# One transformer block on one core: a new order of all steps with 585 filler matmuls in place of 428

## The chip, the cores and the metric

The kernel runs on one core of one Trainium2 chip. The metric is the device time of one execution in microseconds (us). Before the change three runs gave 725.46, 726.37 and 730.91 us, median 726.37. Times taken from a profile are of one further, profiled execution.

## The reference

Sixteen sequences of 256 tokens with 128 features go through two layers, each followed by a residual sum and a layer norm without weights. The first is causal attention with 16 query heads of size 8 over 4 key heads, RMS norm and rotary embedding on q and k, and a soft cap of the scores. The second is a whole block: layer norm, full attention with 16 heads over the 256 tokens, a residual, a second norm, and a mixture of 8 experts of which each token takes the one with the largest gate logit.

```python
scores = jnp.tanh(scores / CAP) * CAP                  # first layer, causal, CAP = 50
y = softmax(where(causal, scores, -inf)) @ v @ w_o
x = _layernorm(x + y)
...
hn2 = _layernorm(x2, ln2_g, ln2_b)                     # second layer, x2 = x + attention
idx = jnp.argmax(hn2 @ gate_w + gate_b, axis=-1)
mid = relu(einsum('th,ehf->etf', hn2, w1) + b1)
moe = (einsum('etf,efh->eth', mid, w2) + b2)[idx, arange]
out = _layernorm(x + (x2 + moe))
```

## The kernel before

**The work.** One step of the outer structure is one sequence, called batch n here (16 of them, two tiles of 128 tokens each). The work of a batch is cut into about 130 named steps. The letter of a name is the stage: a_ loads x, projects q, k, v, and normalises and rotates them; b_ makes the first scores, tanh, exp and the causal mask in six pieces; c_ multiplies by v, projects, adds x and norms; d_ projects q, k, v of the second layer and finds each row's maximum score (d_mx on TensorE, d_max on VectorE, eight pieces); e_ makes the second scores and exp in eight pieces; f_ multiplies by v, projects, norms, picks the expert and computes each token's place in a table sorted by expert, and scatters the rows there (f_scatter, an indirect DMA on GpSimd). A plan (p_plan) after batches 7, 11, 14 and 15 then deals out 9, 8, 6 and 17 tiles of 128 rows of one expert each. The g_ steps do one such tile s of 40: g_row fetches its rows, g_w the expert's first weights, g_hT, g_up, g_mid and g_down compute the two matmuls around a ReLU, g_z, g_rs, g_y norm and g_out scatters the result to the output.

**The order.** Each engine has a program of its own: VectorE (DVE), ScalarE (ACT), GpSimd (POOL), TensorE (PE) and SyncE (SP), which issues most DMAs. The table `ORDER` gives each step of each batch a rank. `batch_order` sorts all ranks into one global list, and `pipeline` on each engine goes through it and emits those steps that the engine has. So the table fixes the order of every engine, and the engines meet only through semaphores; nothing on an engine is run before what stands ahead of it.

**Waiting.** TensorE's results go through two rings of two PSUM banks each, ring_p and ring_s. A step takes the next bank of its ring (`claim`), after the step that used it two turns earlier has been read. Attention outputs go to out1 and out2 instead. On GpSimd stand the powers for the RMS norm (a_pow, L1411), for the layer norms (c_pow L1435, f_pow L1460, g_rs L1484), the stacking of heads (L1414) and the causal masks (L1430).

**Fillers.** A step `w_fill` is a matmul of ones into the bank that the next user of ring_p will take, after claiming it; nothing reads its result. It is one matmul of 256 columns on the full array (L701), or, where the last real matmuls were in columns of 32, four of them (L698). The old table has 428 such steps.

**Row fetches.** g_row waits on SP for its plan. The first fetch of each plan also waits until the last two batches' scatters of that plan have landed, the last plan's for the pad rows too. SP also carries the loads of x (a_load), the row maxima into the operand of the e_ scores (d_m, four small DMAs a batch, L632), the weights (g_w) and the pad stores (q_sp, L666).

Of the kernel before, what the change touches and what calls it, by code (L numbers as in the profile page):

```python
# [18 lines left out]
T = S // P  # L19
# [87 lines left out]
def wait_turn(eng, sem, n, buffers, each):  # L107
# [16 lines left out]
    "a_load": (0, 3, 5, 6, 15, 246, 410, 500, 593, 824, 927, 1050, 1226, 1468, 1509, 1684),  # L124
    "a_xTc": (1, 13, 19, 113, 189, 293, 424, 584, 703, 864, 1002, 1187, 1346, 1511, 1634, 1815),
    "a_xT": (2, 7, 17, 70, 165, 257, 392, 534, 693, 865, 987, 1153, 1292, 1497, 1620, 1785),
    "a_qkv": (4, 12, 64, 128, 224, 377, 506, 652, 822, 984, 1093, 1265, 1422, 1593, 1776, 1898),
    "a_rope": (8, 18, 69, 134, 234, 387, 511, 657, 820, 986, 1114, 1270, 1440, 1607, 1791, 1920),
    "a_sum": (9, 20, 81, 139, 245, 389, 513, 665, 842, 1003, 1143, 1272, 1477, 1617, 1805, 1924),
    "w_fill": (10, 29, 30, 42, 49, 60, 67, 88, 99, 100, 112, 136, 152, 154, 159, 164, 169, 181, 185, 197, 202, 203,  # L130
# [198 lines left out]
def post_ln_block(nc, x, w_q, w_k, w_v, w_o, ln1_g, ln1_b, ln2_g, ln2_b, wq, bq, wk, bk, wv, bv, wo, bo,  # L329
                  gate_w, gate_b, w1, b1, w2, b2, c_rope, c_square, c_small, out):  # L330
    with ExitStack() as ctx:
# [250 lines left out]
        for j, (name, n) in enumerate(order):  # L582
# [3 lines left out]
            elif name[:4] in TILE_SHAPE:  # L586
                shape = TILE_SHAPE[name[:4]]
            elif name in ON_TENSOR or name[:4] in ("b_sc", "d_mx", "e_sc"):
                shape = "full"

        def bank(name, n):
            k = ring_of(name, n)
            return ring[k][turn[name, n] % RINGS[k]]
# [927 lines left out]
```

## Time and profile before

| | |
|---|---|
| median of three runs | 726.37 us |
| their spread | 725.46 to 730.91 us |
| span of the profiled execution, first to last instruction | 701.0 us |
| TensorE busy, mean granted clock | 570.1 us (81%), 0.927 |
| VectorE, ScalarE, GpSimd busy | 480.9, 425.4, 416.7 us |
| DMA | 34.30 MB |

The profile gives the span alone; the median of the runs lies 25.4 us above it, which is what lies around the instructions. Busy time of TensorE is of matmuls that overlap in a pipeline. The granted clock is a share of 2.4 GHz: 1.0 is that level, 0.5 is 1.2 GHz. In the chain of waits each piece is what the one after it waited for, or the instruction before it on the same engine. Times of a stretch are microseconds from the start of the span.

### The profile page before, as it was taken

The page shows a single profiled execution, that of the slowest core. Times are in us where ns is not written, and L with a number is a line of the kernel's source. Part 1 is how long each engine was busy: PE and PEld are TensorE (multiplying, and loading weights), DVE is VectorE, ACT ScalarE, POOL GpSimd, SP SyncE. Part 2 cuts the span into 40 slices and gives each one's busy share as a digit, 9 for nine tenths or more (in the row PEclk, how much of TensorE's full clock was granted, in tenths as well). Part 3 has the DMA queues.
Part 4 walks back from the last instruction along what each step waited for, and adds up shares of the span by engine and source line. Part 5 has one row for each costly group of instructions (what it writes and reads, how often), then busy time and mean ns, then how long its engine had stood idle before and what let it go on. Part 6 is the DMA issues. An engine that isn't in the chain of part 4 may idle for free.

```text
span 701.0 us, 16358 instructions
## 1 busy us (share of the span) xinstructions
PE 570.1 (81%) x5771; PEld 339.1 (48%) x5771; DVE 480.9 (69%) x1356; ACT 425.4 (61%) x650; POOL 416.7 (59%) x443
## 2 busy tenths in 40 slices
PE   2648888888888878888897898878997899888992
PEld 1324333344445444455454554545553555557992
DVE  3546757868678868587867768687777787635452
ACT  1675376676785666757677596756675654534661
POOL 2469573648486953775757585769544235525664
PEclk9969779899999988799999999899998999999996
DMA  6420000000000100000012301001002022186650
GB/s 146 135 69 2 8 1 9 2 24 1 9 2 25 40 2 6 5 16 10 17 41 62 85 9 36 1 20 60 25 29 62 12 69 91 39 257 183 187 149 6
DMA packets 30143, 34.30 MB, mean 49 GB/s; under 512 B 6970, under 2 KB 21984, under 8 KB 30064
## 3 DMA queue, kind: packets, MB, share of 16 engines
q1 hardware_dynamic: 26096, 25.53, 12.9%
q0 software_dynamic: 2816, 6.43, 2.6%
q10 hardware_dynamic: 1152, 1.30, 0.6%
q8 instruction: 47, 0.77, 0.5%
q14 instruction: 32, 0.26, 0.1%
HBM read 22.37 MB, written 11.27 MB: 48 GB/s over the span
## 4 chain that ended last, share of the span: by engine, by line
PE 40%; DVE 23%; POOL 16%; issue 10%; ACT 7%; SPq 2%; DMA 1%; POOLq 0%; ACTq 0%; DVEq 0%
DVE mx L1230 10%; PE out L877 6%; POOL rs L1411 5%; PE ring_s L863 3%; POOL stack L1414 3%; PE out L762 3%; PE ring_p L943 3%; PE ring_p L701 3%; PE ring_s L843 3%; POOL p L1430 2%; ACT p L1004 2%; PE ring_p L814 2%; ACT p L973 2%; PE ring_s L749 2%; PE ring_p L931 1%
## 5 line engine op out<-in xcount | busy, mean ns | idle before, releaser
L1230 DVE TENSOR_REDUCE mx<-ring_s 128x4 f32<-128x1024 f32 x128 | 152.8, 1218 | 26.9 <-PE ring_s L843 26.1
L1004 ACT ACTIVATE p<-ring_s 128x1024 f32<-128x1024 f32 x128 | 126.3, 1027 | 38.8 <-PE ring_s L863 38.3
L973 ACT ACTIVATE p<-ring_s 128x1024 f32<-128x1024 f32 x96 | 97.1, 1022 | 38.5 <-PE ring_s L749 38.1
L1411 POOL TENSOR_TENSOR rs<-ms,small 128x40 f32<-128x40 f32 x14 | 94.8, 6772 | 27.6 <-DVE ms L1093 27.3
L1414 POOL TENSOR_SCALAR stack<-stack 128x256 f16<-128x256 f16 (+1 forms) x96 | 65.0, 700 | 75.7 <-DVE stack L1222 42.8
L1430 POOL TENSOR_SCALAR_AFFINE_SELECT p<-p 128x512 f32<-128x512 f32 (+1 forms) x96 | 75.8, 798 | 56.4 <-ACT p L977 56.3
L977 ACT ACTIVATE p<-p 128x1024 f32<-128x1024 f32 x96 | 100.2, 1057 | 0.7
L701 PE MATMUL ring_p<-blank 128*128 128x256 f16 x362 | 80.6, 286 | 5.1 <-ACT t_midT L1037 1.9
L877 PE MATMUL out<-p,v 128*32 128x256 f32 x1024 | 69.8, 400 | 1.3 <-DVE rb L1288 1.2
L843 PE MATMUL ring_s<-kc,qs 32*128 32x256 f16 x512 | 51.2, 281 | 20.2 <-DVE mx L1230 13.0
L863 PE MATMUL ring_s<-qs,kc 32*128 32x256 f16 x512 | 49.4, 290 | 10.1 <-DMA qs<-mT 4.5
L1489 POOL DMA_INDIRECT out<-t_y,t_idx x40 | 41.3, 1034 | 16.4 <-DVE t_y L1380 9.0
L701 PEld LDWEIGHTS ring_p<-blank 128*128 128x128 f16 x362 | 32.6, 103 | 37.9 <-issue 25.3
L762 PE MATMUL out<-p,v 128*32 128x256 f32 x512 | 47.0, 443 | 4.5 <-POOL p L1430 4.1
L749 PE MATMUL ring_s<-qs,kT 32*128 32x512 f16 x192 | 40.0, 422 | 9.7 <-DVE mx L1230 4.5
L1484 POOL TENSOR_TENSOR t_rs<-t_ve,small 128x1 f32<-128x1 f32 x40 | 23.5, 591 | 35.8 <-DVE t_idx L1375 35.5
L943 PE MATMUL ring_p<-w_down,t_midT 128*128 x320 | 44.0, 283 | 0.0
L1478 POOL DMA_INDIRECT routed_rows<-row,pos x32 | 32.9, 1027 | 15.4 <-issue 8.1
L877 PEld LDWEIGHTS out<-p,v 128*32 128x32 f32 x1024 | 29.1, 112 | 26.1 <-issue 11.9
L943 PEld LDWEIGHTS ring_p<-w_down,t_midT 128*128 128x128 f32 x320 | 40.5, 199 | 0.0
L843 PEld LDWEIGHTS ring_s<-kc,qs 32*128 32x128 f16 x512 | 15.3, 94 | 51.7 <-DVE mx L1230 26.4
L1037 ACT ACTIVATE t_midT<-ring_p,b_up 128x128 f32<-128x128 f32 x92 | 26.3, 368 | 21.7 <-PE ring_p L931 20.1
(162 smaller groups left out, 1111.5 us busy)
## 6 DMA issues: line engine op xcount, KB each, us to landing
w_up<-in_L_ffn_w SPq DMA_DIRECT2D x40, 256.0 KB, 2.8
t_row<-routed_rows SPq DMA_DIRECT2D x40, 132.0 KB, 2.4
routed_rows<-padrow SPq DMA_DIRECT2D x8, 396.0 KB, 3.2
xs<-in_L_attn_x SPq DMA_DIRECT2D x16, 128.0 KB, 2.2
routed_rows<-padrow SPq DMA_DIRECT2D x8, 132.0 KB, 1.9
qs<-mT SPq DMA_DIRECT2D x64, 2.0 KB
out<-t_y,t_idx POOLq DMA_INDIRECT x40, 2.4
b_down<-in_L_ffn_b SPq DMA_DIRECT2D x1, 512.0 KB, 4.8
```

Source lines behind the costliest of these rows:

```text
L701: nc.tensor.matmul(spare[:, 0:256], blank[:, 0:P], blank[:, 0:256], start=True, stop=True)
L843: mm = nc.tensor.matmul(bank(f"d_mx{j}", n)[:, z * 512 + g * S:z * 512 + (g + 1) * S], qs2[32 * i:32 * i + 32, n % 2, 2 * k + g, t * P:(t ...
L863: mm = nc.tensor.matmul(bank(f"e_sc{u}", n)[:, j * 512 + v * S:j * 512 + (v + 1) * S], kc2[32 * i:32 * i + 32, n % 2, g, keys * P:(keys + ...
L877: mm = nc.tensor.matmul(out2[32 * c:32 * c + 32, half * S:(half + 1) * S], v2[:, n % 2, keys, 8 * half + 2 * c + v, :], p2[:, u, at:at + S ...
L943: mm = nc.tensor.matmul(bank("g_down", s)[:, 0:D], t_midT[:, s % 2, c * P:(c + 1) * P], w_down[:, bass.ds(e * FF + c * P, D)], start=False ...
L973: nc.scalar.activation(p1[:, u], bank(f"b_sc{u}", n)[:], ACT.Tanh, scale=float(ISQ / CAP)).then_inc(b_s.sem, 1)
L977: nc.scalar.activation(p1[:, u], p1[:, u], ACT.Exp, scale=CAP).then_inc(b_x.sem, 1)
L1004: nc.scalar.activation(p2[:, u], bank(f"e_sc{u}", n)[:], ACT.Exp, scale=float(ISQ)).then_inc(e_s.sem, 1)
L1230: nc.vector.tensor_reduce(mx2[:, t, 2 * pair:2 * pair + 2, 2 * k:2 * k + 2], bank(f"d_mx{j}", n)[:].rearrange("p (z g s) -> p z g s", z=2, ...
L1411: nc.gpsimd.tensor_tensor(rs1[:], ms1[:], half, ALU.pow).then_inc(a_p.sem, 1)
L1414: return nc.gpsimd.tensor_scalar(dst, src, 1.0, None, ALU.mult)
L1430: nc.gpsimd.affine_select(out=w, in_=w, compare_op=ALU.is_ge, fill=0.0, base=0, pattern=[[0, w.shape[1]], [1, P]], channel_multiplier=-1). ...
```

## The change

The whole of `ORDER` is replaced. The 2415 real steps are the same, with other ranks; the fillers are 585 instead of 428, 524 of them on the full array and 61 in columns. The list of a fetch's scatters is now taken from the order: every g_row waits for the latest two f_scatter steps ahead of it, where only the first of a plan waited for fixed ones. All line numbers behind the table are 7 higher, and in the engines' programs 13 or 14 higher: L701 becomes L714, L698 becomes L711.

```diff
-    "w_fill": (10, 29, 30, 42, 49, 60, 67, 88, 99, 100, 112, 136, 152, 154, 159, 164, 169, 181, 185, 197, 202, 203,
...
+    "w_fill": (1, 2, 3, 4, 5, 6, 12, 13, 14, 18, 19, 20, 21, 22, 23, 29, 30, 31, 32, 33, 34, 35, 36, 37, 38, 39, 40,
...
+        scattered, so_far = {}, []
+        for name, n in order:
+            if name == "f_scatter":
+                so_far.append(n)
+            elif name == "g_row":
+                scattered[n] = tuple(so_far)
...
                 sp.wait_ge(r_v.sem, r_v.upto(k, "row"))
+                for n in scattered[s][-2:]:
+                    wait_turn(sp, rows_out[n % 2], n, 2, 16 * T)
                 if s == PLANS[k][1]:
-                    last = PLANS[k][0]
-                    for n in (last - 1, last):
-                        wait_turn(sp, rows_out[n % 2], n, 2, 16 * T)
                     if k >= LAST:
```

The order of TensorE at the very start, before: transposes of x (ring_p<-ident,xs), projections (w_qkv,xT), the stacked heads' transposes (identh,stack) and first scores (qs,kT).

```order
L707 MATMUL ring_p<-ident,xs 128x128 x2
L714 MATMUL ring_p<-w_qkv,xT 128x192 x2
L707 MATMUL ring_p<-ident,xs 128x128 x2
L701 MATMUL ring_p<-blank 128x256
L714 MATMUL ring_p<-w_qkv,xT 128x192 x2
L707 MATMUL ring_p<-ident,xs 128x128 x2
L725 MATMUL ring_p<-identh,stack 128x128 x8
L733 MATMUL ring_p<-identh,stack 128x128 x2
L749 MATMUL ring_s<-qs,kT 128x512 x4
```

The same stretch after:

```order
L714 MATMUL ring_p<-blank 128x256 x6
L720 MATMUL ring_p<-ident,xs 128x128 x2
L714 MATMUL ring_p<-blank 128x256 x3
L727 MATMUL ring_p<-w_qkv,xT 128x192 x2
L714 MATMUL ring_p<-blank 128x256 x6
L720 MATMUL ring_p<-ident,xs 128x128 x2
L714 MATMUL ring_p<-blank 128x256 x13
L727 MATMUL ring_p<-w_qkv,xT 128x192 x2
L714 MATMUL ring_p<-blank 128x256 x6
L738 MATMUL ring_p<-identh,stack 128x128 x8
```

Fillers stand ahead of the first transpose and between all of these steps, 35 before the first scores where one stood; the third transpose of x has moved behind the scores.

TensorE between the last product with v of batch 0 (`ob`, the transposes of its sums, is the step after it) and the first transpose for the second layer (ident,xh), before:

```order
L775 MATMUL out<-ident,sums 128x128 x4
L749 MATMUL ring_s<-qs,kT 128x512 x2
L781 MATMUL out<-ident,o 128x128 x2
L701 MATMUL ring_p<-blank 128x256
L749 MATMUL ring_s<-qs,kT 128x512 x4
L786 MATMUL out<-w_out,oT 128x128 x2
L749 MATMUL ring_s<-qs,kT 128x512 x2
L701 MATMUL ring_p<-blank 128x256 x2
L808 MATMUL ring_p<-ident,xh 128x128 x2
```

After, from the step behind those transposes of the sums:

```order
L714 MATMUL ring_p<-blank 128x256 x13
L794 MATMUL out<-ident,o 128x128 x2
L714 MATMUL ring_p<-blank 128x256 x6
L762 MATMUL ring_s<-qs,kT 128x512 x4
L714 MATMUL ring_p<-blank 128x256
L799 MATMUL out<-w_out,oT 128x128 x2
L714 MATMUL ring_p<-blank 128x256 x3
L762 MATMUL ring_s<-qs,kT 128x512 x2
L714 MATMUL ring_p<-blank 128x256 x6
L762 MATMUL ring_s<-qs,kT 128x512 x2
L714 MATMUL ring_p<-blank 128x256 x6
L821 MATMUL ring_p<-ident,xh 128x128 x2
```

The real steps are nearly the same, the fillers went from 3 to 35 here (and six column fillers stand just ahead of the piece).

TensorE in the last stage, from the output projection of batch 15 (w_out,oT) over the expert matmuls of two tiles (t_hT,w_up) to its gate (w_gate,h2T), before:

```order
L786 MATMUL out<-w_out,oT 128x128 x2
L701 MATMUL ring_p<-blank 128x256
L931 MATMUL ring_p<-t_hT,w_up 128x128 x8
L701 MATMUL ring_p<-blank 128x256
L897 MATMUL out<-ident,row 128x128 x2
L924 MATMUL ring_p<-ident,t_row 128x128
L701 MATMUL ring_p<-blank 128x256
L903 MATMUL out<-w_gate,h2T 128x8 x2
```

After:

```order
L799 MATMUL out<-w_out,oT 128x128 x2
L944 MATMUL ring_p<-t_hT,w_up 128x128 x8
L714 MATMUL ring_p<-blank 128x256 x9
L910 MATMUL out<-ident,row 128x128 x2
L714 MATMUL ring_p<-blank 128x256 x5
L937 MATMUL ring_p<-ident,t_row 128x128 x2
L916 MATMUL out<-w_gate,h2T 128x8 x2
```

Nine fillers stand where one did ahead of the transposes of `row`, five behind them, and one more expert tile's transpose is ahead of the gate.

## Rows read from the trace of the kernel before

**Rows 1.** The page: span; busy us, share and instructions; clock in 40 slices.

```profile
span 701.0 us, 16358 instructions
...
PE 570.1 (81%) x5771; PEld 339.1 (48%) x5771; DVE 480.9 (69%) x1356; ACT 425.4 (61%) x650; POOL 416.7 (59%) x443
...
PEclk9969779899999988799999999899998999999996
```

**Rows 2.** The page: the chain that ended last, by engine and line.

```profile
PE 40%; DVE 23%; POOL 16%; issue 10%; ACT 7%; SPq 2%; DMA 1%; POOLq 0%; ACTq 0%; DVEq 0%
DVE mx L1230 10%; PE out L877 6%; POOL rs L1411 5%; PE ring_s L863 3%; POOL stack L1414 3%; PE out L762 3%; PE ring_p L943 3%; PE ring_p L701 3%; PE ring_s L843 3%; POOL p L1430 2%; ACT p L1004 2%; PE ring_p L814 2%; ACT p L973 2%; PE ring_s L749 2%; PE ring_p L931 1%
```

**Rows 3.** Length, busy PE, PEld, DVE, ACT, POOL, clock of low-clock stretches; fourteen in the sum.

```profile
41.90:55.50 13.60, 5.95 (x31) 2.66 (x29) 4.55 (x14) 7.31 (x9) 11.20 (x8) 0.50 0.26 89
72.60:82.90 10.30, 9.76 (x63) 3.90 (x67) 7.89 (x10) 2.31 (x4) 7.80 (x11) 0.50 0.01 2
...
sum 92.40, PE 79.73 PEld 41.06 DVE 53.21 ACT 49.35 POOL 56.50; mean PE 5.70 PEld 2.93 DVE 3.80 ACT 3.52 POOL 4.04
```

**Rows 4.** The chain between 72.6 and 82.9 us, by engine and line.

```profile
by line: PE ring_p L814 27.7%; PE ring_s L843 21.6%; PE out L762 21.5%; PE ring_p L701 12.5%; DVE mx L1230 11.9%; PE out L767 8.3%; PE ring_p L808 6.0%; issue 0.4%
```

**Rows 5.** TensorE's waits (us in total, times, longest), and the busy times after 690 us.

```profile
PE ring_s L843 <- DVE mx L1230: 13.0, 22, 1.6
PE ring_s L863 <- DMA qs<-mT: 4.5, 5, 1.4
...
690.00:701.00 11.00, 0.00 (x0) 0.00 (x0) 1.35 (x7) 0.00 (x0) 2.66 (x3) 0.52 0.00 0
```

**Rows 6.** The fillers: groups by line, one burst of two, a piece of the chain.

```profile
L701 PE MATMUL ring_p<-blank 128*128 128x256 f16 x362 | 80.6, 286 | 5.1 <-ACT t_midT L1037 1.9 <-DVE qs L1134 1.3 <-ACT t_hT L1027 0.7
...
L698 PE MATMUL ring_p<-blank 128*32 128x256 f16 x264 | 16.7, 291 | 0.1
...
24.91 0.61 PE L701 MATMUL ring_p<-blank 128*128 128x256 f16 x2
...
602.31 0.76 PE ring_p L701 x7
```

**Rows 7.** TensorE in order of time, from the start; all engines from 25 us.

```profile
9.13 0.69 PE L707 MATMUL ring_p<-ident,xs 128*128 128x128 f32 x2 [9.13 <-DMA w_qkv<-in_L_attn_w_v]
10.28 1.65 PE L714 MATMUL ring_p<-w_qkv,xT 128*128 128x192 f32 x4 [0.46 <-ACT xT L968]
15.90 0.69 PE L707 MATMUL ring_p<-ident,xs 128*128 128x128 f32 x2 [3.98 <-DMA xs<-in_L_attn_x]
...
17.05 1.65 PE L714 MATMUL ring_p<-w_qkv,xT 128*128 128x192 f32 x4 [0.25 <-ACT xT L968]
...
21.83 1.03 PE L725 MATMUL ring_p<-identh,stack 128*128 128x128 f16 x8 [2.70 <-POOL stack L1414]
...
26.58 0.61 PE L749 MATMUL ring_s<-qs,kT 32*128 32x512 f16 x2 [0.31 <-ACT p L973]
...
35.12 0.39 PE L749 MATMUL ring_s<-qs,kT 32*128 32x512 f16 x2
...
25.00:30.00 5.00, 2.66 (x9) 0.44 (x9) 2.35 (x9) 5.00 (x6) 2.29 (x5) 1.00 0.14 51
```

**Rows 8.** GpSimd and TensorE in order of time, 42 to 52 us.

```profile
42.59 6.79 POOL L1411 TENSOR_TENSOR rs<-ms,small 128x40 f32<-128x40 f32 x1 [1.69 <-DVE ms L1093]
49.36 1.00 POOL L1435 TENSOR_TENSOR rl<-ve,small 128x4 f32<-128x4 f32 x1
...
51.82 0.69 PE L808 MATMUL ring_p<-ident,xh 128*128 128x128 f32 x2 [7.65 <-DVE xh L1189]
```

**Rows 9.** TensorE in order of time, 622 to 627 us.

```profile
622.91 1.95 PE L931 MATMUL ring_p<-t_hT,w_up 128*128 128x128 f32 x16
625.45 0.28 PE L701 MATMUL ring_p<-blank 128*128 128x256 f16 x1 [0.59 <-ACT t_midT L1037]
626.42 0.44 PE L897 MATMUL out<-ident,row 128*128 128x128 f32 x2 [0.69 <-DVE row L1189]
```

More of the change, by code:

```diff
@@ L123 @@
 ORDER = {
[L124 to L129, printed above, removed]
@@ new lines @@
+    "a_rope": (16, 43, 103, 202, 311, 464, 618, 775, 959, 1106, 1264, 1403, 1585, 1747, 1912, 2023),
+    "a_sum": (17, 44, 111, 211, 317, 491, 619, 779, 975, 1123, 1287, 1425, 1586, 1748, 1925, 2035),
+    "a_root": (25, 66),
+    "a_split": (26, 70, 150, 259, 357, 537, 672, 826, 1015, 1204, 1341, 1507, 1647, 1792, 1960, 2097),
+    "a_stack": (27, 80, 181, 269, 359, 546, 680, 827, 1026, 1205, 1345, 1512, 1671, 1833, 1979, 2112),
+    "a_qT": (51, 83, 191, 276, 363, 576, 696, 857, 1047, 1225, 1366, 1539, 1687, 1834, 1985, 2128),
@@ new lines @@
+    "d_qT": (216, 331, 442, 633, 788, 968, 1132, 1262, 1408, 1582, 1775, 1938, 2036, 2199, 2386, 2525),
+    "p_bT": (217,),
+    "d_qTc": (222, 343, 458, 642, 804, 979, 1141, 1273, 1417, 1584, 1785, 1939, 2042, 2206, 2387, 2528),
+    "d_kT": (225, 338, 446, 635, 799, 974, 1133, 1270, 1411, 1599, 1779, 1942, 2043, 2213, 2395, 2531),
+    "p_bTc": (228,),
+    "d_kTc": (232, 344, 459, 641, 812, 980, 1139, 1274, 1418, 1606, 1783, 1949, 2052, 2224, 2402, 2535),
[16 rows of a table added]
+    "d_nm": (291, 412, 579, 710, 904, 1068, 1201, 1348, 1492, 1670, 1871, 2055, 2166, 2339, 2453, 2582),
@@ new lines @@
+    "f_scatter": (681, 738, 877, 1065, 1253, 1291, 1454, 1590, 1867, 2161, 2230, 2241, 2443, 2546, 2638, 2741),
+    "p_plan": (1574, 2243, 2633, 2734),
+    "g_w": (1603, 1629, 1602, 1914, 1601, 1915, 1728, 1777, 1693, 2389, 2447, 2248, 2250, 2478, 2286, 2288, 2479,
+        2647, 2648, 2657, 2654, 2695, 2658, 2739, 2740, 2744, 2793, 2792, 2822, 2790, 2823, 2833, 2862, 2835, 2868,
+        2876, 2875, 2898, 2940, 2966),
+    "g_row": (1605, 1627, 1628, 1692, 1726, 1727, 1729, 1763, 1776, 2249, 2251, 2252, 2287, 2361, 2371, 2382, 2388,
+        2639, 2649, 2655, 2656, 2688, 2696, 2742, 2745, 2791, 2796, 2797, 2820, 2828, 2834, 2836, 2861, 2863, 2865,
+        2874, 2892, 2895, 2916, 2964),
@@ new lines @@
+    "g_hT": (1634, 1636, 1793, 1853, 1855, 1972, 2032, 2084, 2227, 2326, 2414, 2462, 2502, 2515, 2567, 2568, 2605,
+        2682, 2683, 2719, 2721, 2732, 2764, 2775, 2801, 2804, 2817, 2819, 2838, 2853, 2866, 2880, 2887, 2903, 2912,
+        2922, 2929, 2939, 2951, 2974),
+    "g_hTc": (1651, 1653, 1798, 1854, 1873, 1981, 2038, 2096, 2246, 2328, 2436, 2466, 2509, 2520, 2572, 2579, 2617,
+        2686, 2691, 2723, 2729, 2736, 2776, 2777, 2803, 2814, 2824, 2832, 2840, 2855, 2873, 2885, 2900, 2905, 2917,
+        2925, 2933, 2946, 2957, 2978),
@@ new lines @@
+    "g_rs": (1801, 1872, 1998, 2027, 2160, 2178, 2221, 2242, 2486, 2495, 2545, 2585, 2596, 2635, 2652, 2671, 2700,
+        2731, 2751, 2766, 2779, 2795, 2799, 2827, 2842, 2847, 2858, 2878, 2889, 2896, 2908, 2918, 2930, 2943, 2952,
+        2959, 2968, 2973, 2986, 2997),
+    "g_y": (1830, 1958, 2091, 2126, 2197, 2202, 2223, 2260, 2489, 2499, 2549, 2597, 2601, 2640, 2666, 2679, 2743,
+        2749, 2752, 2768, 2785, 2800, 2815, 2829, 2845, 2860, 2870, 2882, 2894, 2909, 2915, 2924, 2936, 2950, 2955,
+        2967, 2972, 2976, 2987, 2998),
@@ L308 @@
+    "g_out": (1885, 1997, 2162, 2132, 2284, 2302, 2301, 2283, 2505, 2507, 2637, 2653, 2636, 2726, 2737, 2689, 2765,
+        2781, 2754, 2780, 2794, 2821, 2848, 2841, 2871, 2877, 2888, 2890, 2897, 2910, 2941, 2944, 2942, 2953, 2960,
+        2971, 2975, 2977, 2988, 2999),
+    "q_sp": (2693,),
 }
```

146 lines of the change are left out of this document (56 added, 90 removed), and 184 rows, old and new, of the table ORDER.

## The prediction

> **What bounds the kernel now.** I read the page's shares first, then the chain that ended last, then the stretches of low clock, then TensorE's waits.
>
> No engine is full: over the span of 701.0 us TensorE is busy 81% and ScalarE 61% [rows 1]. The chain changes engine all the time: 40% of it is TensorE, 23% VectorE, 16% GpSimd, and 10% is "issue", the small steps between them [rows 2]. So the time is set by the order in which steps meet, with TensorE the most frequent link.
>
> TensorE's clock is granted at the lower of its two levels (0.50, which is 1.2 of 2.4 GHz) in fourteen stretches before the tail. Together they are 92.4 us long, and TensorE is busy in 79.7 us of them [rows 3]. In the one from 72.6 to 82.9 us the chain is nearly all TensorE: its six TensorE entries sum to 97.6% [rows 4]. In the one from 41.9 to 55.5 us TensorE is busy 5.95 of 13.6 us and GpSimd 11.2, so a faster TensorE buys little there. TensorE's idle time is 131 us (701.0 less 570.1), most of it in short waits such as 22 on the row maxima, 13.0 us in all [rows 5]. About 24 us of it are the wait for the first inputs, 9.13 us, the wait for the second x, 3.98 us [rows 7], and the eleven us after the last matmul [rows 5].
>
> **The change, part by part.**
>
> *Fillers: the count.* The program has 428 filler steps before (362 on the full array, 66 in columns of four matmuls) and 585 after (524 and 61, counted in the order of the steps). They stand in 179 bursts after, 270 before; 34 bursts of the new order have exactly six, and three have thirteen. Before, full ones took 80.6 us and the column ones 16.7 us [rows 6]. One more in a burst costs 0.109 us at full clock (seven in 0.76 us) and about 0.21 at half (two end 0.22 us later than one would: 0.61 against 0.39) [rows 6]. So 162 more full ones are 17.7 us at the full clock, 34 at half; five fewer column ones give back about 1. What of this lies on the path: L701 is 3.0% of the span on the chain by the answer behind [rows 2], 21.0 us of its 80.6, or 26%. By that share the new ones cost 0.26 x 17.7 = 4.6 us. The bounds are 0 (every one in a true wait) and 17.7 (none).
>
> *The start.* Six fillers now stand ahead of the first transpose, behind the same wait for w_qkv that ends at 9.13 us [rows 7]. They run at the half clock: the first 35 us show no change of clock and the column says 1.00, but two L749 matmuls take 0.61 us at 26.58 and 0.39 at 35.12 [rows 7]. Six by 0.21 is +1.3 us on the path, since everything of batch 0 follows from that transpose. Three more stand before L714, whose wait was 0.46 us: 0.63 less 0.46 is +0.2. The thirteen ahead of the second L714 take 2.8 us in place of 0.25 us of waiting; but the first tile's stack has to be built meanwhile (TensorE waits 2.70 us for it before L725 [rows 7]), and the second tile is not wanted on ScalarE before the first is through. I charge nothing for them, 1.5 us as the upper bound. The start: +1.5 us.
>
> *What a faster TensorE gives back at the start.* ScalarE is busy for the whole of 25 to 30 us (5.00 of 5.00) [rows 7], so matmuls that run at full clock 15 us earlier shorten nothing there: 0. The Trainium skill ("TensorE: Matmul & The Clock Gate", section "What's actually happening") says that the lower clock is the default and that activity lifts it. The trace agrees: the first matmuls are slow by the durations. By that rule alone the 39 fillers ahead of the third transpose would bring the higher level forward, and half of the matmul time between some 20 and 35 us, about 4 us, could be saved if ScalarE were not full.
>
> *The hole from 42 to 52 us.* Before, TensorE stands idle 7.65 us before L808, behind GpSimd's 6.79 us power and the 1.00 us one queued after it [rows 8]. The new order puts 44 fillers between the last product with v of batch 0 and its projection for the second layer, where 3 stood: 38 full ones are 4.1 us, six column ones 1.5 (16.7/66 each), in about 9 us of waits, so they fit. On VectorE the sum of squares of batch 2 now goes ahead of batch 0's normalisation, so the power that waits for that sum can start sooner by the normalisation's two instructions, but one mask now stands between it and the next power. I cost this at 0. What is gained is that the clock does not fall here.
>
> *Clock.* All 79.7 us at full speed would be half as long: 39.9 us is the upper bound. How much of it is on the path: TensorE holds 40% of the chain at large and 97.6% in the stretch of [rows 4], but little in the first, where GpSimd holds it; I take 60%, 48 us, and halved that is 24. I take it that 60% of the low time goes, 14 us, and not all of it, since between the third batch's transposes and the last maxima of batch 0, where the second stretch fell, the new order has hardly a filler. A third of this is lost to VectorE and ScalarE, which become late next (the maxima hold up TensorE already [rows 5]). The clock: -10 us, between 0 and -40.
>
> *Order.* 2415 real steps keep their work and their dependencies; they move by some 10 to 20 places. The burst sizes show that the order was made with durations near those of the trace: nine fillers (1.0 us) now stand between L931 and L897, where TensorE had one filler (0.28), 0.59 and 0.69 us of waiting [rows 9]. The fetches of rows 20 and 21 and of the weights 19, 20 and 22 now come ahead of the eight pad stores on SP's queue, not behind them. No instruction is added by this, and the last batch still leaves 20 of the 40 expert tiles behind it. What there is to win is 131 - 24 = 107 us of scattered waits, of which an order can win or lose a part: I bound it at 15 us each way and take -5, since bursts fit waits wherever I compared them.
>
> *Row fetches.* Each now waits for the latest two scatters ahead of it in the order. In this order they are always those that its plan already required (6 and 7, then 10 and 11, 13 and 14, 14 and 15), which the first fetch of each plan waited for before too. Behind it on SP stand weight fetches and the 64 small stores of the maxima (4.5 us of waits on them [rows 5]); none waits longer. Cost 0; a microsecond per plan, 4 in all, if the count were one scatter later.
>
> Sum against the profiled span: +4.6 + 1.5 - 10 - 5 = -8.9, some -9 us (adding the column ones back changes it by 0.3), 692. The median of the runs lies 25.4 us over the span, and nothing of the change touches what lies around it: 726.4 - 9 = 717.
>
> **The rivals.**
>
> *Fillers in the way (slower).* A filler is queued in TensorE's order, and it claims the next bank of ring_p: it cannot be skipped when the step behind it is ready early. If the waits for which the bursts were sized are longer than the true ones in the middle of the kernel, where most steps are, the new ones all go on the path: +17.7, the start +1.5, and at most -5 from the clock with nothing from the order: +14, 740. The point from which it decides: once more than about 70% of the new time is on the path while the low stretches shrink by less than a fifth. For it: L701 is already 21 us of the chain. Against it: the fit in [rows 9], and fewer bursts than before.
>
> *A draw.* The low stretches shift and don't shrink (they followed waits on maxima and on GpSimd that no burst of six covers), or VectorE takes all of the gain: -3 + 4.6 + 1.5 = +3; with up to -8 from the order that is 721 to 729, middle 726.
>
> *The clock stays up throughout.* -24 of the clock, -9 of the order, +6.1 for fillers and start: -27, 699. Against it: the same long waits on the 6.8 us powers remain.
>
> *The change doesn't do what it says* in its third part only: the fetches wait for nothing new. That is in my sum already.
>
> **How the numbers follow.** 1% of 726 is 7.3 us, about what a measurement of this kernel can tell from no change. The forecast's own case (711 to 721, middle 717) has 0.36, the clock that stays up 0.12, the draw 0.24, fillers in the way 0.28. Of the forecast's case a tenth, the side of 719 to 721, counts as the same, and of the slower case a tenth too: faster 0.32 + 0.12 = 0.44, same 0.24 + 0.04 + 0.03 = 0.31, slower 0.25. The range leaves a tenth at either end: 696 to 740.
>
> **What would show it.** Right: fewer than 50 us of low clock before the tail; L808's first wait of 7.65 us gone into fillers; the mean of L701 nearer 0.27 us than 0.29; the first transpose still at 9 us but the first score step 1.5 us later; TensorE's busy time about the same or lower although it has 157 fillers more. Wrong: a chain with L714's full filler (its new line) over 5%; low stretches of the same total; or waits of VectorE and ScalarE on TensorE grown. If SP shows a wait for rows_out ahead of fetches 9 or 17 that delays a store of maxima, my zero for the row fetches is wrong.

## The result and the profile after

The kernel after takes 654.79 us (median of four runs, 654.16 to 655.28) against 727.48 us for the kernel before in the same set (725.46 to 730.91): a ratio of 0.9007, 95% interval 0.8977 to 0.9037. It is 73 us faster. Forecast were 717, and a range of 696 to 740: the sign was right, the size about eight times too small (9 us of 73).

The page of the kernel after, which answers to [rows 1] and [rows 2]:

```profile
span 652.3 us, 16677 instructions
...
PE 566.8 (87%) x5913; PEld 351.3 (54%) x5913; DVE 486.9 (75%) x1356; ACT 423.2 (65%) x650; POOL 419.0 (64%) x443
...
PEclk9697588899899999798999999999999999999997
...
PE 44%; DVE 18%; issue 10%; POOL 9%; ACT 6%; SPq 6%; DMA 5%; POOLq 0%; ACTq 0%; DVEq 0%
DVE mx L1243 6%; PE out L890 5%; POOL rs L1424 4%; PE ring_s L856 4%; PE ring_p L714 4%; PE out L775 4%; PE ring_s L876 3%; PE ring_p L956 3%; PE ring_p L827 3%; PE ring_s L762 3%; ACT p L986 2%; SPq L646 2%; ACT p L1017 2%; DMA qs<-mT 2%; PE ring_p L834 2%
```

The engines do the same work in a shorter span, and their busy times hardly change: VectorE is busy 486.9 us, where it was 480.9, GpSimd 419.0 (416.7), and TensorE 566.8 (570.1) although it runs 157 more filler steps. What went is waiting. TensorE's idle time fell from 131 to 85.5 us. In the chain the share of GpSimd fell from 16% to 9%, that of the maxima (mx) from 10% to 6%. The first of these is not steady: the same two programs profiled again have 11% (before_again) and 13% (after_again). SyncE and the DMAs together rose from 3% of the chain to 11% (6% in after_again).

A first correction of the reading of before belongs here. The profiled execution of after has a span of 652.3 us and a time of 654.2: some 2 us lie outside the span, not 25. The profile of before was of a quicker execution than any of its three timed runs. Its 701.0 us would suit the chips on which whole sets of before have medians near 703 us; on which chip it was taken isn't on record. The repeat of before below has a span of 721.7 and a time of 723.4 us, and in other sets the same program had medians from 702.8 to 727.4. So the comparisons of times below are ratios to before on the same chip, or between runs of one chip, unless it is said otherwise.

The low-clock stretches of after ahead of its tail, in the columns of [rows 3], all nine:

```profile
18.20:21.60 3.40, 3.38 (x15) 2.37 (x12) 3.16 (x11) 0.00 (x0) 0.88 (x2) 0.50 1.06 293
25.00:35.30 10.30, 7.58 (x48) 3.21 (x52) 4.26 (x16) 9.52 (x12) 5.21 (x8) 0.50 0.03 12
52.30:59.10 6.80, 5.64 (x26) 2.60 (x26) 4.26 (x8) 2.54 (x3) 6.00 (x9) 0.50 0.00 0
66.00:83.00 17.00, 14.33 (x88) 7.06 (x92) 12.32 (x23) 10.85 (x14) 14.15 (x12) 0.50 0.01 1
93.30:103.50 10.20, 9.54 (x74) 3.90 (x77) 5.31 (x14) 9.13 (x10) 9.48 (x4) 0.50 0.31 100
...
sum 68.10, PE 60.11 PEld 28.73 DVE 39.48 ACT 44.46 POOL 48.55; mean PE 6.68 PEld 3.19 DVE 4.39 ACT 4.94 POOL 5.39
```

68 us are left of 92, and 48 of them lie in the first 104 us; four short ones follow, and none after 308 us. In the repeat of after below it is 65 us in twelve stretches, three of them behind 555 us.

TensorE's and VectorE's waits in after (us in total, times, longest), beside [rows 5] and [rows 8]:

```profile
PE ring_p L821 <- DVE xh L1202: 7.5, 3, 4.6
PE ring_s L856 <- DVE mx L1243: 4.6, 8, 1.1
PE ring_s L762 <- ACT p L986: 4.2, 4, 2.2
...
PE ring_s L876 <- DMA qs<-mT: 3.4, 5, 1.5
```

```profile
DVE t_z L1379 <- PE ring_p L956: 23.6, 21, 3.8
DVE mx L1243 <- PE ring_s L856: 11.3, 24, 1.1
```

The 22 waits of TensorE on the maxima, 13.0 us, are 8 of 4.6 us. The long hole before the first `xh` is not gone, it is 4.6 us where it was 7.65. The fillers:

```profile
L714 PE MATMUL ring_p<-blank 128*128 128x256 f16 x524 | 89.5, 286 | 17.3 <-DMA w_qkv<-in_L_attn_w_v 9.5 <-DVE t_z L1379 2.6 <-ACT t_hT L1040 2.5
L711 PE MATMUL ring_p<-blank 128*32 128x256 f16 x244 | 9.9, 276 | 1.5 <-DVE sw L1093 1.4
```

A mean of 286 ns, the same as before [rows 6], and 99.4 us in all against 97.3. They hold 4% of the chain (3% before).

### The profile page after: what moved, and what is told of

It reads as the page before. It is cut to its first block, busy times and chain, and to the rows that moved or that the text cites. A ratio compares the mean times of both kernels' runs of the same rounds, so it can differ in the third digit from the quotient of the medians.

```text
span 652.3 us, 16677 instructions
## 1 busy us (share of the span) xinstructions
PE 566.8 (87%) x5913; PEld 351.3 (54%) x5913; DVE 486.9 (75%) x1356; ACT 423.2 (65%) x650; POOL 419.0 (64%) x443
## 4 chain that ended last, share of the span: by engine, by line
PE 44%; DVE 18%; issue 10%; POOL 9%; ACT 6%; SPq 6%; DMA 5%; POOLq 0%; ACTq 0%; DVEq 0%
DVE mx L1243 6%; PE out L890 5%; POOL rs L1424 4%; PE ring_s L856 4%; PE ring_p L714 4%; PE out L775 4%; PE ring_s L876 3%; PE ring_p L956 3%; PE ring_p L827 3%; PE ring_s L762 3%; ACT p L986 2%; SPq L646 2%; ACT p L1017 2%; DMA qs<-mT 2%; PE ring_p L834 2%
## 5 line engine op out<-in xcount | busy, mean ns | idle before, releaser
L1243 DVE TENSOR_REDUCE mx<-ring_s 128x4 f32<-128x1024 f32 x128 | 152.1, 1219 | 12.2 <-PE ring_s L856 11.3
L1017 ACT ACTIVATE p<-ring_s 128x1024 f32<-128x1024 f32 x128 | 125.1, 1031 | 27.8 <-PE ring_s L876 23.5
L986 ACT ACTIVATE p<-ring_s 128x1024 f32<-128x1024 f32 x96 | 97.1, 1026 | 50.8 <-PE ring_s L762 50.3
L714 PE MATMUL ring_p<-blank 128*128 128x256 f16 x524 | 89.5, 286 | 17.3 <-DMA w_qkv<-in_L_attn_w_v 9.5
L714 PEld LDWEIGHTS ring_p<-blank 128*128 128x128 f16 x524 | 47.5, 101 | 45.9 <-issue 19.6
L890 PE MATMUL out<-p,v 128*32 128x256 f32 x1024 | 67.3, 388 | 0.5 <-ACT p L1017 0.5
L856 PE MATMUL ring_s<-kc,qs 32*128 32x256 f16 x512 | 49.6, 277 | 5.8 <-DVE mx L1243 4.6
L762 PE MATMUL ring_s<-qs,kT 32*128 32x512 f16 x192 | 38.3, 417 | 9.7 <-ACT p L986 4.2
L775 PE MATMUL out<-p,v 128*32 128x256 f32 x512 | 44.4, 421 | 0.9 <-POOL p L1443 0.8
L956 PE MATMUL ring_p<-w_down,t_midT 128*128 x320 | 42.3, 275 | 0.0
L890 PEld LDWEIGHTS out<-p,v 128*32 128x32 f32 x1024 | 28.0, 110 | 24.9 <-issue 10.8
L956 PEld LDWEIGHTS ring_p<-w_down,t_midT 128*128 128x128 f32 x320 | 38.9, 192 | 0.0
L1050 ACT ACTIVATE t_midT<-ring_p,b_up 128x128 f32<-128x128 f32 x92 | 26.5, 373 | 16.1 <-PE ring_p L944 13.1
L1497 POOL TENSOR_TENSOR t_rs<-t_ve,small 128x1 f32<-128x1 f32 x40 | 23.6, 591 | 15.3 <-DVE t_idx L1388 13.2
```

Source lines behind the costliest of these rows:

```text
L714: nc.tensor.matmul(spare[:, 0:256], blank[:, 0:P], blank[:, 0:256], start=True, stop=True)
L775: nc.tensor.matmul(out1[32 * c:32 * c + 32, half * S:(half + 1) * S], v1[:, n % 2, 0, i, v, :], p1[:, 3 * half + g, j * 512 + v * S:j * 51 ...
L856: mm = nc.tensor.matmul(bank(f"d_mx{j}", n)[:, z * 512 + g * S:z * 512 + (g + 1) * S], qs2[32 * i:32 * i + 32, n % 2, 2 * k + g, t * P:(t ...
L890: mm = nc.tensor.matmul(out2[32 * c:32 * c + 32, half * S:(half + 1) * S], v2[:, n % 2, keys, 8 * half + 2 * c + v, :], p2[:, u, at:at + S ...
L956: mm = nc.tensor.matmul(bank("g_down", s)[:, 0:D], t_midT[:, s % 2, c * P:(c + 1) * P], w_down[:, bass.ds(e * FF + c * P, D)], start=False ...
L986: nc.scalar.activation(p1[:, u], bank(f"b_sc{u}", n)[:], ACT.Tanh, scale=float(ISQ / CAP)).then_inc(b_s.sem, 1)
```

## The experiments

In the edits `OLD` is the rank table of before, put beside `ORDER` (the new one) into one kernel, and three helpers stand ahead of `batch_order`: `sorted_steps(table)` is the old body of `batch_order`, `real(order)` leaves the w_fill steps out, and `with_fillers(order, source)` puts the fillers that `source` has ahead of a TensorE step ahead of the same step of `order` (later, where ring_p's next bank would not yet have been read: 45 of 428 fillers and 75 of 585, by 2 to 3 TensorE steps in the mean).

**The kernel before again.**

> The kernel before, unchanged, profiled again. The profile that the prediction rests on had a span of 701.0 us and the runs took 725.5 to 730.9 us; in the new kernel the two differ by less than 2 us (652.3 and 654.2). Theory A (about 25 us lie outside the span of the kernel before): span near 701 and a time near 727. Theory B (the profiled execution was simply a quicker one, and time and span agree to 2 us here too): a span of 724 to 729 us, and then the trace shows which wait is longer than in the first profile.

Measured 727.41 us, ratio 1.0013 (0.9971 to 1.0055).

```profile
span 721.7 us, 16358 instructions
```

The low clock ahead of the tail lasts 116 us here and 92 in the first profile. This execution is the fairer base for reading after.

**The order alone, without any filler**, of the old table and of the new:

```diff
 def batch_order():
-    steps = [(rank, name, n) for name, ranks in ORDER.items()
-             for n, rank in zip(ONLY.get(name, range(len(ranks))), ranks)]
-    return [(name, n) for _, name, n in sorted(steps)]
+    return real(sorted_steps(OLD))          # old_none;  new_none: real(sorted_steps(ORDER))
```

> The old order of real steps without any filler. Order theory: 725 to 750 us, that is 60 to 75 us over new_none. Filler theory: the same as new_none within 15 us.

> The new order of the 2415 real steps without any filler. Order theory (the gain is the new order of real steps; fillers are worth little): 655 to 675 us, mean clock down to 0.85 to 0.90. Filler theory (the gain is the clock and the order is a draw, as I had it): 700 us or more, with low-clock stretches of over 200 us in all.

Measured on one chip: old_none 723.12 us, 0.9997 (0.9948 to 1.0046); new_none 676.86 us, 0.9336 (0.9272 to 0.9401). So the order of the real steps alone is worth 46 us, and the old fillers were worth nothing. The busy times between 100 and 560 us, of old_none first and of new_none next (us, TensorE, weight loads, VectorE, ScalarE, GpSimd, clock):

```profile
100.00:560.00 460.00, 372.85 (x3683) 199.27 (x3680) 339.75 (x868) 303.87 (x405) 286.16 (x293) 0.86 0.08 23
```

```profile
100.00:560.00 460.00, 401.58 (x4064) 221.90 (x4060) 377.19 (x961) 323.60 (x447) 302.42 (x310) 0.88 0.10 29
```

In the same 460 us all engines get through more work, VectorE 961 instructions instead of 868. The clock is nearly the same, 0.88 against 0.86, but not quite: over the whole kernel new_none has 164 us of low clock ahead of the tail and old_none 188. TensorE's busy time for the same 5145 matmuls falls with it, from 551.9 to 538.6 us. (The mean clock is higher in each of the four runs of new_none, 0.863 to 0.872, than in any of the ten of old_none, 0.841 to 0.862.) So of the 49 us between the two spans (719.0 and 669.8) 36 are less idle time of TensorE and 13 are faster matmuls. The waits behind it, first of old_none, then of new_none:

```profile
PE ring_s L1079 <- DVE mx L1466: 20.3, 29, 1.6
...
DVE mx L1466 <- PE ring_s L1079: 34.6, 35, 2.8
...
DVE qk L1439 <- PE ring_p L1050: 16.9, 12, 3.1
DVE qs L1370 <- PE ring_p L961: 14.8, 8, 3.8
```

```profile
PE ring_s L893 <- DVE mx L1280: 9.5, 17, 1.3
...
DVE mx L1280 <- PE ring_s L893: 23.6, 32, 2.3
...
DVE qk L1253 <- PE ring_p L864: 6.3, 9, 1.1
DVE qs L1184 <- PE ring_p L775: 5.8, 7, 2.1
```

TensorE waits less for VectorE and VectorE less for TensorE, at the same pairs of steps: 20.3 + 34.6 us at the maxima became 9.5 + 23.6, and the waits of 16.9 and 14.8 us for the second layer's q, k and the first layer's qs became 6.3 and 5.8. It is many waits of about a microsecond each, and no single one is the bound.

**Each set of fillers on the other order.**

```diff
+    return with_fillers(real(sorted_steps(ORDER)), sorted_steps(OLD))    # new_old
+    return with_fillers(real(sorted_steps(OLD)), sorted_steps(ORDER))    # old_new
```

> The new order of real steps with the 428 old fillers, each ahead of the same TensorE step as in the old order (later where its bank could not yet be claimed). Order theory: within 10 us of the new kernel (655), 655 to 665. Filler theory: 690 us or more.

> The old order of real steps with the 585 new fillers, each ahead of the same TensorE step as in the new order (later where its bank could not yet be claimed). Without fillers the old order took 723 us and with its own 727; the new order 677 without, 697 with the old fillers, 655 with its own. Theory that a filler pays by itself (it holds the clock up wherever it stands): 22 us less than without, 700 to 705. Theory that a filler pays only in the wait for which it was sized, and is in the way elsewhere (new_old: +20 us over none): 735 to 750.

Measured: new_old 696.85 us, 0.9596 (0.9536 to 0.9656), 20 us more than new_none on the same chip. That is where the filler theory had it, but for another reason: new_none, with no filler at all, is far below. old_new 736.81 us, 1.0493 (1.0438 to 1.0548), 33 us more than before on its chip (703.63). The chains by engine, of new_old and of old_new:

```profile
PE 52%; DVE 18%; issue 11%; ACT 8%; POOL 4%; DMA 3%; SPq 2%; ACTq 0%; POOLq 0%; DVEq 0%
```

```profile
PE 50%; DVE 21%; POOL 14%; issue 9%; ACT 4%; SPq 1%; DMA 1%; POOLq 0%; ACTq 0%; DVEq 0%
...
DVE mx L1466 9%; PE out L1113 6%; PE ring_p L937 6%; POOL rs L1647 5%; PE out L998 4%; PE ring_p L1179 4%; PE ring_s L1099 4%; PE ring_s L1079 3%; POOL stack L1650 3%; PE ring_p L1050 3%; POOL p L1666 2%; PE ring_s L985 2%; PE ring_p L1167 2%; PE out L1003 2%; PE ring_s L1167 2%
```

TensorE holds half of each chain, and the full fillers (L937 here) 6% of old_new's. Both kernels spend less time at the low clock than their twins without fillers (116 against 164 us, 143 against 188), and lose. The twin of old_new, old_none, ran on another chip, where its ratio to before was 0.9997. This is the rival that I called "fillers in the way", and it is real: but it strikes a set of fillers that was fitted to another order, and the change came with its own.

**Thin fillers**: the same 585, 16 columns instead of 256 (in the column fillers too, whose lines are left out here).

```diff
-                    nc.tensor.matmul(spare[:, 0:256], blank[:, 0:P], blank[:, 0:256], start=True, stop=True)
+                    nc.tensor.matmul(spare[:, 0:16], blank[:, 0:P], blank[:, 0:16], start=True, stop=True)
```

> The new kernel with its 585 fillers at the same places, each matmul of 16 columns in place of 256: same claims of banks and same weight loads, a sixteenth of the columns. Clock theory (a filler pays because it keeps the clock at its higher level): near the new order without fillers, 672 to 680 us where the kernel before takes 726 (ratio 0.925 to 0.94), low-clock stretches over 150 us. Placement theory (it pays by the time at which it lets the next step through): within 4 us of the new kernel.

> The new kernel, unchanged, beside the kernel before on this chip. The kernel before took 725.6 us on one chip and 703.6 on another; the new one took 654.8 beside 727.5. If the difference between chips is a different pattern of low clock that both kernels feel, the ratio stays 0.90. If the new kernel feels it less, since its fillers hold the clock, it stays near 650 us on any chip: 0.92 where the kernel before takes 704.

Measured on one chip: new_thin 681.19 us, 0.9385 (0.9304 to 0.9466); after_again 650.8 us, 0.8955 (0.8898 to 0.9013). new_none had 0.9336. The fillers of new_thin:

```profile
L714 PE MATMUL ring_p<-blank 128*128 128x16 f16 x524 | 39.2, 175 | 16.9 <-DMA w_qkv<-in_L_attn_w_v 9.3 <-DVE t_z L1379 2.9 <-ACT t_hT L1040 2.1
```

```profile
PEclk9987578779779657887959899898997899799997
```

They claim the same banks at the same places, and give nothing: the clock is as low as without fillers (181 us of low clock ahead of the tail, new_none 164, after 68). So what the full fillers give, 0.9336 - 0.8955 or 28 us by this set and 24 by the ratio of the first one, comes by the clock that their work keeps up, and not by the banks that they claim.

**GpSimd's powers and VectorE's maxima made cheap.** The powers are replaced by a multiplication with 1 (another rs, so other numbers), and the maxima are taken over the first half of the keys, in either kernel.

```diff
-                nc.gpsimd.tensor_tensor(rs1[:], ms1[:], half, ALU.pow).then_inc(a_p.sem, 1)
+                nc.gpsimd.tensor_scalar(rs1[:], ms1[:], 1.0, None, ALU.mult).then_inc(a_p.sem, 1)
...
-                                        bank(f"d_mx{j}", n)[:].rearrange("p (z g s) -> p z g s", z=2, g=2),
+                                        bank(f"d_mx{j}", n)[:].rearrange("p (z g s) -> p z g s", z=2, g=2)[:, :, :, 0:P],
```

> The kernel before with the fourteen powers of 40 columns on GpSimd (6.8 us each) replaced by a multiplication by one: the RMS norm's root is left out for batches 2 to 15. GpSimd theory (in the old order steps that others wait for stand queued behind these powers, and the new order moved them off the chain, GpSimd's share of it fell from 11 to 15% to 9%): 680 to 695 us. Alignment theory (the gain comes from TensorE and VectorE meeting with shorter waits, whatever GpSimd does): 710 to 722.

> The same replacement in the new kernel. GpSimd theory: hardly faster, 645 to 653 us, since the powers no longer hold anything up for long. Alignment theory: it gains the same number of us as the old one does.

> The kernel before with each of the 128 row maxima on VectorE taken over the first half of the keys only (the second half is left out of the maximum), 0.6 us each in place of 1.2, some 75 us less of VectorE's work. Alignment theory: in the old order TensorE and VectorE wait for each other by turns (VectorE is busy 74% of the middle stretch, 82% in the new order), so the gain is a small part of the 75 us, 15 to 30 us. If VectorE's rate sets the old order's time: 45 us or more.

> The same halved maxima in the new kernel, where VectorE is closer to full. Alignment theory: the new order has taken the waits between VectorE and TensorE already and TensorE is 93% busy with its fillers, so it gains less than the old one, 5 to 15 us. If VectorE has become the bound: 25 us or more, more than the old one gains.

| | ratio to before on its chip | against its own kernel |
|---|---|---|
| old_cheap_pow | 0.9894 (0.9838 to 0.995) | -8 us |
| new_cheap_pow, 640.35 us | 0.9118 (0.907 to 0.9165) | about -9, of new_sp_old on that chip |
| old_cheap_max | 0.9733 (0.9659 to 0.9807) | -21 us |
| new_cheap_max, 639.64 us | 0.88 (0.8742 to 0.8857) | -11 us, of after_again |

Fourteen powers of 6.8 us are 95 us of GpSimd's time, and taking them away gives 8 us in the old order (3.5 to 11.4 by the interval). In the new one it gives about 9, but only against new_sp_old, whose own four runs lie 9 us apart, since after did not run on that chip. That the new order hides the powers better, which the fall of GpSimd's share of the chain from 16% to 9% suggests, is therefore not where the 46 us came from: there were only some 8 to be had. Of the two that were made cheap the maxima are nearer to a bound, and even they give 21 and 11 us.

**SyncE alone in the old order, and the fetches' wait undone.**

```diff
-        def pipeline(parts):
+        def pipeline(parts, order=order):
...
-            pipeline(dict(a_load=a_load, d_m=d_m, g_row=g_row, g_w=g_w, q_sp=q_sp))
+            pipeline(dict(a_load=a_load, d_m=d_m, g_row=g_row, g_w=g_w, q_sp=q_sp), other)   # new_sp_old; other is sorted_steps(OLD)
...
-                for n in scattered[s][-2:]:
-                    wait_turn(sp, rows_out[n % 2], n, 2, 16 * T)
                 if s == PLANS[k][1]:
+                    last = PLANS[k][0]
+                    for n in (last - 1, last):
+                        wait_turn(sp, rows_out[n % 2], n, 2, 16 * T)                                     # new_old_waits
```

> The new kernel with SyncE's queue alone in the old order (loads, stores of the maxima, fetches of rows and weights), all other engines as in the new one. If the order of the fetches does something of its own: 658 to 670 us. If it does not (my sum had it at 0): 653 to 657.

> The kernel after with the third part of the change undone: the first fetch of each plan alone waits for the scatters, as before. Theory (my prediction: the waits fall on the same scatters, cost 0): the time of the kernel after, 651 to 655 us or 0.895 to 0.90 of the kernel before on the same chip. Rival (the 36 fetches that now wait too hold up what is queued behind them on SyncE, which is 6% of the chain of the kernel after against 2% before): 3 us or more faster, below 648.

Measured: new_sp_old 648.99 us (646.9 to 655.8), ratio 0.9226; new_old_waits 645.33 us (644.1 to 650.4), 0.9202 (0.9152 to 0.9252). Both ran on chips where before takes 703 us, and after itself did not, so neither is told from after: new_no_last, which ran on the chip of new_old_waits, has 650.62 us (645.5 to 653.0). The traces decide more. SyncE's waits for the rows to land, in before, after and new_old_waits:

```profile
SPq L110 <- DMA routed_rows<-row,pos: 15.5, 1, 15.5
```

```profile
SPq L110 <- DMA routed_rows<-row,pos: 8.3, 1, 8.3
...
SPq L664 <- DMA routed_rows<-row,pos: 2.6, 1, 2.6
```

```profile
SPq L110 <- DMA routed_rows<-row,pos: 9.2, 1, 9.2
...
SPq L665 <- DMA routed_rows<-row,pos: 2.6, 1, 2.6
```

L110 is the helper that waits for scatters: one wait in each, and no further one by the new rule. The 2.6 us at L664 and L665 are the last plan's wait for its idle rows, which stands in both kernels. And the first fetch of new_old_waits is issued at 343 us, while its batch 8 was done 5 us ahead of new_no_last before that (its maxima at 321.9 and 326.7 us). At the rank of batch 15 the lead is still 5.4 us (570.1 and 575.5), and from there to the last tile's sum it needs 61.6 us, where after needs 61.1. So what made this run quicker was not the fetches. The clock differs: here are the first 200 us of new_old_waits and of new_no_last, whose programs are the same there.

```profile
0.00:200.00 200.00, 160.61 (x1642) 89.38 (x1645) 138.91 (x339) 127.19 (x156) 128.38 (x130) 0.90 0.13 37
```

```profile
0.00:200.00 200.00, 163.15 (x1601) 89.52 (x1602) 135.76 (x336) 123.69 (x152) 124.06 (x125) 0.85 0.13 37
```

**The expert tiles out of the way.** To see whether the gain is in how expert tiles are threaded into the attention steps, both orders, without fillers, with all g_ steps at the end:

```diff
 def batch_order():
+    base = real(sorted_steps(OLD))          # old_g_last;  new_g_last: ORDER
+    experts = [step for step in real(sorted_steps(ORDER)) if step[0][0] == "g"]
+    return [step for step in base if step[0][0] != "g"] + experts
```

> No fillers; the old order of all steps but those of the 40 expert tiles, which come behind everything else, in both this and new_g_last in the same order. The step that ends the attention work is the last position (pos) of batch 15: 649 us into the old order without fillers, 599 into the new one, both with tiles in between. Interleaving theory (the new order gains by where the tiles stand): here both reach it within 12 us of each other, near 570 us. Attention theory: the old order is still 30 to 45 us behind.

> The same with the new order of the attention steps. Interleaving theory: the end of the attention work and the total time within 12 us of old_g_last. Attention theory: 30 to 45 us sooner in both.

Measured on one chip: 813.12 us, 1.1237 (1.1179 to 1.1295), and 774.1 us, 1.0691 (1.0631 to 1.0752). 39 us of the 46 remain where no expert tile is threaded in, and at the rank of batch 15 the two stand 44 us apart (645.2 and 601.5 us). The gain is among the attention steps. VectorE between 150 and 560 us in old_g_last and new_g_last:

```profile
150.00:560.00 410.00, 326.03 (x3074) 164.49 (x3072) 289.82 (x734) 255.62 (x316) 246.78 (x247) 0.80 0.04 12
```

```profile
150.00:560.00 410.00, 346.35 (x3332) 176.22 (x3333) 319.69 (x802) 269.39 (x333) 256.55 (x258) 0.82 0.04 14
```

**The old order up to batch 7, the new one behind it**, no fillers:

```diff
+    one, two = real(sorted_steps(OLD)), real(sorted_steps(ORDER))
+    first = one[:one.index(("d_mx0", 7))]
+    there = set(first)
+    return first + [step for step in two if step not in there]
```

> No fillers; every step that stands ahead of the first row maximum of batch 7 in the old order comes first, in the old order, then all others in the new order. In the profiles without fillers the old order is 11 us behind the new one at the maxima of batch 7 and 47 at those of batch 15. If each stretch of the order has its own gain: 723 less 37, 684 to 690 us. If the gain hangs on an advance that is built up from the start: 700 us or more.

Measured 689.91 us, 0.9538 (0.9492 to 0.9584), between old_none and new_none. Of the 48 us between those two ratios 33 are there with the new order from batch 7 on alone, so the later part of the order does not need the earlier one for most of its gain. The end of each batch's maxima (the last VectorE step of d_) in us, with the rank of batch 15 and the last tile's sum:

| batch | 0 | 4 | 8 | 12 | 15 | rank 15 | last tile |
|---|---|---|---|---|---|---|---|
| before_again | 85.6 | 220.3 | 355.8 | 512.6 | 617.9 | 651.1 | 711.0 |
| old_none | 84.0 | 216.1 | 350.7 | 509.2 | 612.2 | 649.4 | 708.3 |
| new_none | 86.9 | 215.8 | 339.6 | 477.5 | 564.8 | 598.6 | 659.1 |
| after | 88.1 | 213.0 | 330.0 | 461.7 | 547.0 | 580.5 | 641.6 |

To batch 4 the two orders without fillers are level. From there to batch 15 the new one needs 349 us where the old one needs 396. The tail behind the rank of batch 15 is 59 to 61 us in all four.

**Without the fillers of the start, and without those of the tail.**

```diff
+    kept = [step for j, step in enumerate(order) if step[0] != "w_fill" or not (j < at(("b_sc0", 0)))]     # new_no_start
+    kept = [step for j, step in enumerate(order) if step[0] != "w_fill" or not (j > at(("f_rank", 15)))]   # new_no_last
```

> The new kernel without the 35 fillers ahead of the first scores. By my sum the first six cost 1.3 us and the next three 0.2, and the earlier full clock buys nothing: 1.5 us less, 649 to 652. If the earlier clock is worth more than they cost: 653 to 657.

> The kernel after without the 36 fillers that stand behind the last batch's choice of experts (f_rank of batch 15). The stretch from there to the end was 3.7 us longer after (61.1 us) than before (57.4 us). Theory A (these fillers stand in the way of the last expert tiles): 2 to 4 us faster, 647 to 650, with the stretch back at 57 to 59 us. Theory B (they keep the clock up there and sit in true waits): the same or slower, 651 to 656, the stretch 61 us or more and more low clock in it. Theory C (they cost nothing and save nothing, the stretch is longer for what SyncE and VectorE bring later): the same time, 61 us, no more low clock.

Measured: new_no_start 651.18 us, 0.9018 (0.8976 to 0.906), no better than after (0.9007 and 0.8955). Its first score step starts at 23.97 us, where the two profiles of after have it at 24.94 and 25.13: the fillers cost about 1 us there. How much of it reaches the end of batch 0's maxima can't be told, 84.5 us here but 86.0 and 88.1 in the two profiles of after, which are one program. The end does not see it. new_no_start also has only 44 us of low clock ahead of the tail, against 68 and 65 in those two, and isn't quicker. new_no_last 650.62 us, 0.924 (0.919 to 0.9291): the stretch behind the rank is 65 us long (575.5 to 640.2), not 61 as in after, at a clock of 0.92, where after has 1.00 and after_again 0.94. So the tail's fillers are not in the way. No kernel of these is better than after by more than its runs scatter, and the work left out by the cheap ones can't be left out.

## Why the prediction was wrong

*What bounds the kernel.* "The time is set by the order in which steps meet" was right, and the forecast then did not price it.

*The step that failed: Order, "I bound it at 15 us each way and take -5".* It is -46 (old_none to new_none; -39 without expert tiles in between). The text had a wide enough bound in its hands, 107 us of scattered waits, and cut it to 15 with two reasons that say nothing of the size: that steps move by only 10 to 20 places, and that 20 of 40 tiles are still left behind the last batch. The second is true and was beside the point, the tail is as long as it was. On the first, the shape of the schedule hardly changed: from the first transpose of a batch to its rank there are 777 places before and 762 after (mean of batches 5 to 12), from its first to its last maxima 51 in both. The steps moved even less than the text said: among the real steps the median move is 6 places, and nine in ten move by 20 or less. But with 135 steps to a batch and a period of some 36 us, 6 places are 1.6 us and 15 are 4 us, while the 22 waits on the maxima before had a mean of 0.6 us [rows 5]. A small move in places was as large as the waits that it could remove. This compares sizes; it doesn't show which moves brought the gain. About 36 us of it are less idle time of TensorE. The other 13 are faster matmuls at less low clock, a path from the order to the clock that the forecast didn't have. Even its fastest case, 699, had only 9 us for the order and 24 for the clock.

*Clock and fillers: the direction right, the net too small.* The sum had +4.6 for fillers, +1.5 for the start and -10 for the clock, -4 net; measured 24 to 28 us from new_none to after, with the old fillers worth nothing on their own order. The first term held: L714 has 4% of the chain of 652.3 us, some 25 us, where L701 had 21, +4. The start held within half a microsecond: the first score step moved from 23.94 to 25.13 us, 1.2 for 1.5. The clock was mis-sized because it was read as the difference of two filler sets, 92 to 68 us of low clock in the profiles shown. Against the same order without fillers it is 164 to 68, 96 us less. The low level is half of the high one, so this is worth half of 96 at most, an estimate of 48 us; with the 25 us of fillers on the chain taken off, 23 are left, and the runs give 24 to 28. This fits, but one sum that fits is no proof: for the old order it would be 72 us less of low clock, 36 us, less the 22 of L701 on before_again's chain of 721.7 us, a gain of 14, and before is no faster than old_none (0.9997, interval 0.9948 to 1.0046). And new_no_start, with 35 fillers fewer and 20 to 24 us less of low clock than after, is no quicker. So half of the low time is an upper bound here and no price. The Trainium skill ("TensorE: Matmul & The Clock Gate", section "Terms") prices a low clock at its time by one less the ratio. The last two comparisons show less than that, and the measurement decides. Why the old fillers gave nothing stays open.

*The hole from 42 to 52 us: half right.* Cost 0, and the clock is up through it (35 to 52 us). But it is still a wait of 4.6 us; without any filler it is 5.9 (new_none).

*VectorE and ScalarE late next, "a third is lost".* Not seen for VectorE: its wait for the scores that it takes maxima of fell from 29.8 us (before_again) to 11.3. ScalarE's wait for the second layer's scores fell from 42.5 to 23.5 us, that for the first layer's rose from 44.1 to 50.3. TensorE and VectorE waited less for each other together, which a model that hands one engine's gain to the next engine's bound can't see.

*Row fetches: right.* No new wait.

*The base.* "The median lies 25.4 us above the span, which is what lies around the instructions" was wrong: 2 us lie there. The number 717 does not hang on it (692 is 701 less 9, and 717 is 726 less 9), but a reader should not look for 25 us around a program.

*The rivals.* "Fillers in the way" decided nothing here, and was shown to be worth 20 and 33 us where fillers stand at places fitted to another order. "The clock stays up throughout" was nearest in its number, but its mechanism isn't what happened: 65 to 68 us of low clock are left, and it had the order at 9.

*The list of what would show it.* Right: TensorE's busy time lower with 157 fillers more, the first scores later by 1.2 us where it said 1.5, L714 below 5% of the chain. Wrong: 68 us of low clock instead of under 50, the first transpose at 10.8 us and not at 9 (its own sum put six fillers ahead of it), the 7.65 us not gone but 4.6, L714's mean 286 ns and not near 270. The marks of being wrong did not appear as such, apart from the one wait of ScalarE. Nearly all of the marks were about fillers and the clock, none about the order: the forecast had no check on the term that decided.

**What stays open.** Which of the moved attention steps bring the 46 us. No kernel was run in which VectorE, ScalarE or GpSimd alone goes in the other order; with each engine in an order of its own they might wait for each other in a circle, which wasn't shown either way. The best that was shown is that the gain is spread over batches 5 to 15.

## What to carry to other kernels

When a whole order is replaced, take the bound from the idle time that any order could win, here 107 us, not from how far steps move; and convert places into microseconds before calling a move small. Fillers belong to one order: the new set was worth 24 to 28 us in its own order and cost 33 in the old one, and the old set was worth nothing in its own and cost 20 in the new one. So change both together, and test the order without any fillers to see what is whose. Hold the span of a profile against the time of that same execution, and never against the median of other runs.

## What the runs showed of the hardware

- The same program has different times on different chips: medians of before are 702.8 and 703.6 us in two sets, 722.9 to 727.5 in the others. The kernel after and its near variants differ less, 645 to 655 us. Low clock may go with it: the profile of 701.0 us, whose chip isn't on record, has 92 us of it, that of 721.7 us has 116. But 24 us at half speed can account for 12 of these 21 us at most, by estimate.
- A matmul of 16 columns took 175 ns in the mean at the same places where one of 256 took 286, and kept the clock no higher than no matmul at all (a mean of 0.86 from 100 to 560 us, against 0.88 without fillers and 0.97 with those of 256 columns).
- With the full fillers at the start the record of the clock first says 1.00 at 12.7 to 15.1 us, in all eight executions that have them; without them, and with the thin ones, at 34 to 37 us. It doesn't last: in those eight the first fall to 0.50 comes at 16.1 to 21.9 us.
- The same 5145 matmuls were busy for 551.9 us with 188 us of low clock ahead of the tail and for 538.6 us with 164: 13 us of busy time for 24 us of low clock (old_none and new_none).
